# Value bias taken out of the value rows and added to the residual rows on GpSimd

## The chip, the core and the metric

The kernel runs on one core of one Trainium2 chip. A core has five engines with instruction streams of their own: TensorE (PE, matrix multiplications into PSUM), VectorE (DVE), ScalarE (ACT), GpSimd (POOL) and SyncE (SP, which here issues DMAs). They meet through semaphores. SBUF is the working memory of 128 partitions, PSUM holds eight accumulator banks, and DMAs move data to and from HBM. The metric is device time in microseconds (us) of one execution.

## The reference, cut to what matters

32 images are cut into patches and projected to 192 channels, reordered to 256 tokens along a Hilbert curve, and joined by 77 text tokens: 333 tokens of 192 channels an image (B = 32, L = 333, D = 192). Then:

```python
q = layernorm(h)
key = pointwise(depthwise(q)) + pw_b          # 9 taps, 12 heads of 16 channels
kern = einsum(key * q, ak_w) + ak_b           # 9 scores for each token and head
w = softmax(kern, axis=-1)                    # over the 9 taps: sums to 1
v = q @ pt_w.T + pt_b                         # the values and their bias
vp = pad(v, 4 zero rows on both sides)        # the padding is put on after the bias
out[l] = sum_k w[l, k] * vp[l + k]            # window of 9 tokens
h = h + out
h = h + ffn(layernorm(h))                     # 8 experts, top 2, capacity 1598
```

Since the nine weights sum to one, the bias can be left out of v and added once to h, if the rows of the padding hold minus the bias.

## The kernel before, in words

There are two stages. The second (the experts, from about 785 us) isn't touched. The first has two interleaved parts. Part one works on pairs of images (pair p, 16 pairs; buffers alternate with p % 2): TensorE projects the patches (patch), VectorE adds the token bias and takes statistics (norm), GpSimd makes scale and offset of them (pair_norm), ScalarE normalises (normalise), TensorE transposes, ScalarE copies the transposed tiles out (tiles_out). For each of three tiles t TensorE runs the convolution (conv) and the value projection (values). attend(p, t) on VectorE then adds the pointwise bias and multiplies by the query (L605), and adds the value bias ptb_sb to the one value bank bankV while it moves it to the row buffer (L610). scores and scores_out make the 9 x 12 scores. SyncE stores the row buffer (values, hidden row, scores) in the DRAM tensor token_rows (store).

Part two works on groups of four images (group g, 8 groups, two buffers): load_window reads scores (kb), values with a margin of four rows on both sides (vx) and the hidden rows (hg) back in another layout, 11 tokens to a partition. VectorE runs the softmax (softmax_top L632 to L636, ScalarE's exponential, softmax_end) and the window in two slices of 6 and 5 tokens: for each of nine taps a product (L652) and an addition to hg (L670), so that hg becomes the residual sum. Then statistics, a layer norm through GpSimd (slice_norm) and ScalarE (normalise_slice), halves in 16 bits (high_parts on ScalarE, low_parts on GpSimd), the router (logits, top_two, counts_before, offsets, places) and 22 indirect DMAs a group that GpSimd issues (scatter).

No planner sets the order: each engine's program is written out by hand in one loop over it = 0 to 7, in which it handles pairs 2 it and 2 it + 1, the softmax of group it - 1 and the tail of group it - 2. VectorE fills the time between two attends with pieces of the window (part). Each engine takes its instructions strictly in that order, so a wait holds up all that stands behind it. The margins of token_rows are written once from the tile zeros by three DMAs that ScalarE issues; the same engine issues fill(0) and fill(1), 16 large DMAs that preset the expert slots, in iteration 0.

In the last iteration the group 7 has no pairs beside it: TensorE sums the first slice's taps (L1015, L1019), and GpSimd's order is low_parts(6, 0), scatter(5, 0), slice_norm(6, 1), scatter(5, 1) and so on.

## Time and profile before

| | us |
|---|---|
| median of 3 runs | 1483.41 (1480.34 to 1488.11) |
| profiled execution, time | 1478.12 |
| profiled execution, span | 1476.2 |
| busy PE, DVE, ACT, POOL | 1249.6, 991.2, 449.7, 715.1 |

Busy times are sums over the whole span; shares differ much between the two stages, so stretches are read one by one. In rows of instructions, the first number is the start in us from the span's start, the second the busy time (of all merged into the row), then engine, line and operation, output and inputs, shape, and how many instructions were merged; in brackets stands how long the engine had been idle before and what released it. An engine name with a q (ACTq, SPq) is its issuing side. L12 is line 12 of the kernel.

### The profile page before, as it was taken

What the parts mean: (1) busy time and instruction counts of PE and PEld (TensorE: products, weight loads), DVE (VectorE), ACT (ScalarE), POOL (GpSimd) and SP (SyncE); (2) the same over time, 40 slices, a digit from 0 to 9 for tenths busy, and PEclk for the clock granted to TensorE, in tenths of its full rate; (3) what the DMA queues carried; (4) which work ended last, traced back from release to release, by engine and by line L of the source; (5) the groups of instructions that cost most, each with busy time, mean ns of one, the idle gap of its engine ahead of it and who ended that gap; (6) DMA issues with size and microseconds to landing.
All of it is one profiled execution on the core that took longest, in us unless ns stands there. A gap on an engine that the chain in (4) does not pass through costs nothing. (4 is left out here: it accounts for less than half of the span.)

```text
span 1476.2 us, 23362 instructions
## 1 busy us (share of the span) xinstructions
PE 1249.6 (85%) x8476; PEld 991.4 (67%) x8476; DVE 991.2 (67%) x1924; ACT 449.7 (30%) x949; POOL 715.1 (48%) x545
## 2 busy tenths in 40 slices
PE   6969888988989798843640999999999999999994
PEld 6757666777767576533330787787777778877873
DVE  4107959999999999997841565656564655656552
ACT  2011222223232222212031443434442434344331
POOL 1000221766666665746376345545556255455455
PEclk9989998999989898765755999999999999999997
DMA  9795563655656554623024455464656365554533
GB/s 328 299 357 154 134 175 87 183 150 158 180 161 171 153 139 110 155 74 100 23 69 122 84 79 89 62 111 55 103 61 106 58 100 64 91 78 61 71 46 36
DMA packets 224279, 178.52 MB, mean 121 GB/s; under 512 B 128872, under 2 KB 208006, under 8 KB 224160
## 3 DMA queue, kind: packets, MB, share of 16 engines
q1 hardware_dynamic: 176896, 117.16, 32.7%
q0 software_dynamic: 37248, 36.15, 16.1%
q10 hardware_dynamic: 10016, 23.66, 4.3%
q8 instruction: 70, 1.15, 0.3%
q14 instruction: 49, 0.40, 0.1%
HBM read 69.22 MB, written 89.23 MB: 107 GB/s over the span
## 5 line engine op out<-in xcount | busy, mean ns | idle before, releaser
L1127 POOL DMA_INDIRECT out<-yb,meta x200 | 329.4, 1647 | 323.2 <-DVE yb L1184 252.2
L1216 DVE TENSOR_TENSOR hidden<-silu,bankU 128x320 f32<-128x320 f32 x320 | 155.2, 487 | 198.0 <-PE bankU L1249 172.7
L902 PE MATMUL bankK<-normedT,conv_w 128*128 128x333 f32 x864 | 278.7, 471 | 0.0
L85 POOL DMA_INDIRECT expert_inputs<-slot_rows,slots x176 | 230.0, 1307 | 78.4 <-issue 55.0
L1156 ACT ACTIVATE silu<-bankG 128x320 f32<-128x320 f32 x320 | 139.8, 437 | 379.7 <-PE bankG L1249 358.4
L902 PEld LDWEIGHTS bankK<-normedT,conv_w 128*128 128x128 f32 x864 | 169.5, 202 | 78.0 <-issue 13.1
L1262 PE MATMUL bankY<-w_high,hidden_high 128*128 128x192 f16 x800 | 197.2, 246 | 0.0
L1263 PE MATMUL bankY<-w_low,hidden_high 128*128 128x192 f16 x800 | 197.2, 246 | 0.0
L1264 PE MATMUL bankY<-w_high,hidden_low 128*128 128x192 f16 x800 | 197.2, 246 | 0.0
L652 DVE TENSOR_TENSOR prod<-window_values,kb 128x960 f32<-128x960 f32 (+1 forms) x135 | 168.3, 1255 | 3.6
L670 DVE TENSOR_TENSOR hidden_group<-hidden_group,prod 128x960 f32<-128x960 f32 (+1 forms) x135 | 169.1, 1253 | 0.5
L352 POOL TENSOR_TENSOR tmp<-mean_var,pool_constants 128x6 f32<-128x6 f32 (+1 forms) x32 | 25.3, 791 | 250.5 <-DVE mean_var L597 230.2
L880 PE MATMUL bankH<-wp_sb,patches 128*128 128x192 f32 x768 | 131.6, 333 | 10.1 <-DMA tokb_sb<-in_tokb 10.1
L880 PEld LDWEIGHTS bankH<-wp_sb,patches 128*128 128x128 f32 x768 | 128.2, 195 | 10.1 <-DMA tokb_sb<-in_tokb 10.1
L1207 DVE TENSOR_TENSOR hidden_low<-hidden,hidden_high 128x640 f16<-128x640 f32 x160 | 131.6, 822 | 2.2
L1245 PE MATMUL bankG<-xeT,w_high 128*128 128x320 f16 x320 | 96.3, 301 | 39.8 <-DMA xeT<-expert_inputs 36.3
L1150 ACT CAST hidden_high<-hidden 128x640 f16<-128x640 f32 x160 | 115.0, 719 | 8.8 <-DVE hidden L1216 8.8
L1184 DVE TENSOR_SCALAR yb<-bankY,slot_weight 128x192 f32<-128x192 f32 x200 | 75.8, 413 | 62.2 <-PE bankY L1264 62.0
L1245 PE MATMUL bankU<-xeT,w_high 128*128 128x320 f16 x320 | 96.3, 301 | 4.6 <-DVE hidden L1216 4.6
L1248 PE MATMUL bankG<-xeT,w_high 128*128 128x320 f16 x320 | 96.4, 301 | 0.0
L1246 PE MATMUL bankG<-xeT,w_high 128*128 128x320 f16 x320 | 96.4, 301 | 0.0
L1247 PE MATMUL bankG<-xeT,w_low 128*128 128x320 f16 x320 | 96.3, 301 | 0.0
(131 smaller groups left out, 2212.7 us busy)
## 6 DMA issues: line engine op xcount, KB each, us to landing
patches<-in_x SPq DMA_DIRECT2D x16, 1536.0 KB, 8.6
token_rows<-rowbuf SPq DMA_DIRECT2D x32, 492.0 KB
expert_inputs<-prod ACTq DMA_DIRECT2D x8, 1470.0 KB, 15.0
window_values<-token_rows SPq DMA_DIRECT2D x32, 264.0 KB, 5.5
hidden_group<-token_rows SPq DMA_DIRECT2D x32, 264.0 KB, 7.1
expert_inputs<-prod ACTq DMA_DIRECT2D x8, 980.0 KB, 16.6
window_values<-token_rows SPq DMA_DIRECT2D x32, 192.0 KB, 5.7
kb<-token_rows SPq DMA_DIRECT2D x32, 148.5 KB, 4.7
```

The costliest lines, as they stand in the source:

```text
L85: nc.gpsimd.indirect_dma_start(out=xslots[:, :], out_offset=bass.IndirectOffsetOnAxis(ap=idx[g % 2][:, k, r:r + 1], axis=0), in_=xrow[g % ...
L652: return V.tensor_tensor(to[:, 0:(hi - lo) * D].rearrange("p (a d) -> p a d", d=IPG), vx[g % 2][:, (lo + k) * D:(hi + k) * D].rearrange("p ...
L670: added[k] = done(V.tensor_tensor(acc, acc, prod[k % 2][:, 0:(hi - lo) * D], ALU.add))
L880: mm = T_.matmul(bankH[c][:, m * D:(m + 1) * D], xb[u][:, m, kc * TI + c * 128:kc * TI + c * 128 + 128], wp_sb[:, kc, :], start=(kc == 0), ...
L902: mm = T_.matmul(bankK[(u + t) % 2][:, 0:L], conv_w[:, t // 2, k, :], qT[u][:, t, k:k + L], start=(k == 0), stop=(k == K - 1))
L1127: nc.gpsimd.indirect_dma_start(out=out[:, :], out_offset=bass.IndirectOffsetOnAxis(ap=meta[t % NMETA][:, c, 0:1], axis=0), in_=yb[v][:, c, ...
L1156: nc.scalar.activation(sg[m][:, :], bankG[m][:, 0:HALF], ACT.Silu, scale=1 / WSCALE).then_inc(silu_done, 1)
L1216: V.tensor_tensor(hf[j % 2][:, m * HALF:(m + 1) * HALF], sg[m][:, :], bankU[m][:, 0:HALF], ALU.mult).then_inc(prod_done, 1)
L1245: T_.matmul(o, wh[ee][:, lo:lo + 128], high, start=True, stop=False)
L1262: T_.matmul(o, hh[v][:, j, cs], wh[ee][:, ws], start=(j == 0), stop=False)
L1263: T_.matmul(o, hh[v][:, j, cs], wl[ee][:, ws], start=False, stop=False)
L1264: mm = T_.matmul(o, hl[v][:, j, cs], wh[ee][:, ws], start=False, stop=(j == NJ - 1))
```

## The change

The bias leaves attend: VectorE no longer touches the value bank. values_out on ScalarE copies it (three for each pair, at six places of ScalarE's loop). The margin rows are filled with minus the bias, which VectorE writes into the tile zeros first; their three DMAs move from the front of ScalarE's program to iteration 0, behind the first tile copies. bias_rows(g) on GpSimd adds the bias to the 11 residual rows of each partition, in place, once hg is loaded; VectorE's first window addition and, in the last group, TensorE wait for it. GpSimd waits for the constants before its first work. The bias constant is loaded once instead of twice side by side.

```diff
--- before.py
+++ after.py
@@ -101,7 +101,7 @@
             akB_sb = sb("akB_sb", [128, 2 * HB * K])
             ptA_sb = sb("ptA_sb", [128, D])
             ptB_sb = sb("ptB_sb", [128, 2 * D])
-            ptb_sb = sb("ptb_sb", [128, 2 * D])
+            ptb_sb = sb("ptb_sb", [128, D])
             conv_w = sb("conv_w", [128, 2, K, 128])
             xb = [sb(f"patches{u}", [128, 2, KC * TI]) for u in range(2)]
             rowb = [sb(f"rowbuf{u}", [128, 3, 2, ROW]) for u in range(2)]
@@ -168,7 +168,7 @@
             const_loaded = sem("const_loaded")
             zeroed = sem("zeroed")
             empty_set = sem("empty_set")
-            margins_done = sem("margins_done")
+            margin_set, margins_done = sem("margin_set"), sem("margins_done")
             fill_done = sem("fill_done")
             x_loaded = [sem(f"x_loaded{u}") for u in range(2)]
             txt_loaded = [sem(f"txt_loaded{u}") for u in range(2)]
@@ -192,6 +192,7 @@
 
             vk_loaded = [sem(f"vk_loaded{b}") for b in range(2)]
             hg_loaded = [sem(f"hg_loaded{b}") for b in range(2)]
+            hg_biased = sem("hg_biased")
             step = sem("vector_step")
             sc_ready, sc_exp = sem("sc_ready"), sem("sc_exp")
             weights_done = sem("weights_done")
@@ -211,7 +212,7 @@
 
             CONSTS = [(idn[:, :], ident), (wp_sb[:, :, :], wpatch), (tokb_sb[:, :], tokb), (dw_sb[:, :, :], dw),
                       (pw_sb[:, :, :], pw), (pwb_sb[:, :], pwb), (akA_sb[:, :], akA), (akB_sb[:, :], akB),
-                      (ptA_sb[:, :], ptA), (ptB_sb[:, :], ptB), (ptb_sb[:, :], ptb),
+                      (ptA_sb[:, :], ptA), (ptB_sb[:, :], ptB), (ptb_sb[:, :], ptb[:, 0:D]),
                       (akb_sb[:, :], akb), (wgA[:, :], wg[0:128, :]), (wgP[:, :], wgpair), (wgC[:, :], wg[D2:D, :]), (low_sb[:, :], lower),
                       (rev[:, :], revrank), (val[:, :], valid), (sbase[:, :], slotbase), (tid[:, :], tokid)]
             NFIRST = 3
@@ -389,9 +390,19 @@
                         pool.wait_ge(scattered, 16 * NSC * (g + 1))
                         pool.sem_inc(rows_sent, 1)
 
+                def bias_rows(g):
+
+                    pool.wait_ge(hg_loaded[g % 2], loads(g, 1))
+                    nc.gpsimd.tensor_tensor(hg[g % 2][:, :, :], hg[g % 2][:, :, :],
+                                            ptb_sb[:, :].unsqueeze(1).to_broadcast([128, R, D]), ALU.add)\
+                        .then_inc(hg_biased, 1)
+
+                pool.wait_ge(const_loaded, NCONST)
                 pair_norm(0)
                 for it in range(NG):
                     pair_norm(2 * it + 1)
+                    if it:
+                        bias_rows(it - 1)
                     if it > 1:
                         low_parts(it - 2, 0)
                     if it > 2:
@@ -407,6 +418,7 @@
                     if it:
                         slice_norm(it - 1, 0)
                 low_parts(NG - 2, 0)
+                bias_rows(NG - 1)
                 scatter(NG - 3, 0)
                 slice_norm(NG - 2, 1)
                 scatter(NG - 3, 1)
@@ -423,15 +435,6 @@
             def _(act):
                 for dst, src in CONSTS[NFIRST:]:
                     act.dma_start(dst, src).then_inc(const_loaded, 16)
-                act.wait_ge(zeroed, 1)
-                act.dma_start(rows[:, 0:PAD, :], zeros[0:B].unsqueeze(1).to_broadcast([B, PAD, ROW]))\
-                   .then_inc(margins_done, 16)
-                tail = LROWS - PAD - L
-                act.dma_start(rows[:, PAD + L:LROWS, :], zeros[0:B].unsqueeze(1).to_broadcast([B, tail, ROW]))\
-                   .then_inc(margins_done, 16)
-                act.dma_start(out[N:N + 2 * SLOT_TILE, :].rearrange("(p j) d -> p j d", p=CHUNK),
-                              zeros[0:CHUNK, 0:D].unsqueeze(1).to_broadcast([CHUNK, 2 * SLOT_TILE // CHUNK, D]))\
-                   .then_inc(margins_done, 16)
                 tiles = xslots.rearrange("(e t p j) f -> e p t (j f)", t=TPE, p=CHUNK, e=E)
 
                 def fill(q):
@@ -441,6 +444,26 @@
                             act.dma_start(tiles[e][:, v::2, :], prod[v][:, 0:EMPTY].bitcast(u16).unsqueeze(1)
                                           .to_broadcast([CHUNK, (TPE + 1 - v) // 2, SLOT_TILE // CHUNK * XW]))\
                                .then_inc(fill_done, 16)
+
+                def margins():
+
+                    act.wait_ge(margin_set, 1)
+                    act.dma_start(rows[:, 0:PAD, :], zeros[0:B].unsqueeze(1).to_broadcast([B, PAD, ROW]))\
+                       .then_inc(margins_done, 16)
+                    tail = LROWS - PAD - L
+                    act.dma_start(rows[:, PAD + L:LROWS, :], zeros[0:B].unsqueeze(1).to_broadcast([B, tail, ROW]))\
+                       .then_inc(margins_done, 16)
+                    act.dma_start(out[N:N + 2 * SLOT_TILE, :].rearrange("(p j) d -> p j d", p=CHUNK),
+                                  zeros[0:CHUNK, D:2 * D].unsqueeze(1).to_broadcast([CHUNK, 2 * SLOT_TILE // CHUNK, D]))\
+                       .then_inc(margins_done, 16)
+
+                def values_out(p, t):
+                    u, T = p % 2, CT[t]
+                    act.wait_ge(v_ready, 3 * p + t + 1)
+                    if t == 0:
+                        wait(act, row_stored[u], 64 * (p // 2))
+                    nc.scalar.copy(rowb[u][0:T, t, :, 0:D],
+                                   bankV[0:T, 0:2 * D].rearrange("p (m d) -> p m d", m=2)).then_inc(v_evac, 1)
 
                 def normalise(p):
                     u = p % 2
@@ -515,18 +538,28 @@
                 tiles_out(0)
                 for it in range(NG):
                     p = 2 * it
+                    if it == 0:
+                        margins()
+                    values_out(p, 0)
+                    values_out(p, 1)
                     normalise(p + 1)
                     if it == 0:
                         act.wait_ge(empty_set, 2)
                         fill(0)
+                    values_out(p, 2)
                     if it:
                         exponentials(it - 1)
                     tiles_out(p + 1)
                     scores_out(p)
                     if it > 1:
                         normalise_slice(it - 2, 1)
+                    values_out(p + 1, 0)
                     if it > 1:
-                        routing_out(it - 2, 0, NQ)
+                        routing_out(it - 2, 0, 3)
+                    values_out(p + 1, 1)
+                    if it > 1:
+                        routing_out(it - 2, 3, NQ)
+                    values_out(p + 1, 2)
                     if not last(p + 1):
                         normalise(p + 2)
                     if it == 0:
@@ -605,13 +638,6 @@
                     V.scalar_tensor_tensor(ca[u][:, t, :], bankK[(u + t) % 2][:, 0:L],
                                            pwb_sb[:, t // 2:t // 2 + 1], qT[u][:, t, PAD:PAD + L],
                                            ALU.add, ALU.mult).then_inc(ca_done, 1)
-                    T = CT[t]
-                    dve.wait_ge(v_ready, 3 * p + t + 1)
-                    V.tensor_tensor(rowb[u][0:T, t, :, 0:D],
-                                    bankV[0:T, 0:2 * D].rearrange("p (m d) -> p m d", m=2),
-                                    ptb_sb[0:T, :].rearrange("p (m d) -> p m d", m=2), ALU.add)\
-                        .then_inc(v_evac, 1)
-
 
                 counted = [0]
 
@@ -674,7 +700,7 @@
                         mult(k)
                         yield
                         if k == 1:
-                            dve.wait_ge(hg_loaded[g % 2], loads(g, 1))
+                            dve.wait_ge(hg_biased, g + 1)
                         add(k - 1)
                         yield
                     add(K - 1)
@@ -778,6 +804,7 @@
                 dve.wait_ge(first_loaded, 16 * NFIRST)
                 norm(0)
                 dve.wait_ge(const_loaded, NCONST)
+                V.tensor_scalar(zeros[:, 0:D], ptb_sb[:, :], -1.0, None, ALU.mult).then_inc(margin_set, 1)
                 for t in range(2):
                     for k in range(K):
                         ins = V.tensor_scalar(conv_w[:, t, k, :], pw_sb[:, t, :], dw_sb[:, t, k:k + 1], None, ALU.mult)
@@ -848,7 +875,7 @@
                         dve.wait_ge(tap_summed, k - 1)
                     tap(g, 0, k, prodL[k % 2]).then_inc(tap_made, 1)
                     if k == 1:
-                        dve.wait_ge(hg_loaded[g % 2], loads(g, 1))
+                        dve.wait_ge(hg_biased, g + 1)
                     if k == 3:
                         top_two(h)
                     if k == 6:
@@ -1007,7 +1034,7 @@
                 g, h = NG - 1, NG - 2
                 for _ in logits(h, NPAIR):
                     pass
-                pe.wait_ge(hg_loaded[g % 2], loads(g, 1))
+                pe.wait_ge(hg_biased, g + 1)
                 pe.wait_ge(ca_done, 3 * NPAIR)
                 pe.wait_ge(h_in_rows, 2 * NPAIR)
                 hgf = hg[g % 2][:, :, :].rearrange("p r d -> p (r d)")
```

## Rows read from the trace of the kernel before

**Rows 1.** The page's 40 slices of the span, VectorE, busy tenths.

```profile
DVE  4107959999999999997841565656564655656552
```

**Rows 2.** VectorE's waits, 200 to 760 us: total us, times, longest us.

```profile
DVE conv_attn L605 <- PE bankK L902: 14.7, 2, 13.3
...
DVE rowbuf L610 <- PE bankV L916: 3.0, 5, 1.1
```

**Rows 3.** VectorE's instructions in order of time, iteration 6 and behind the loop.

```profile
503.50 0.56 DVE L605 SCALAR_TENSOR_TENSOR conv_attn<-bankK,pwb_sb,normedT 128x333 f32<-128x333 f32 x1
...
511.29 1.40 DVE L632 TENSOR_TENSOR kb<-kb,akb_sb 128x1188 f32<-128x1188 f32 x1 [0.23 <-DMA window_values<-token_rows]
512.72 1.39 DVE L634 TENSOR_REDUCE kmax<-kb 128x132 f32<-128x1188 f32 x1
514.15 2.60 DVE L636 TENSOR_TENSOR kb<-kb,kmax 128x1188 f32<-128x1188 f32 x1
...
517.14 0.54 DVE L610 TENSOR_TENSOR rowbuf<-bankV,ptb_sb 77x384 f32<-77x384 f32 x1
517.61 1.14 DVE L670 TENSOR_TENSOR hidden_group<-hidden_group,prod 128x960 f32<-128x960 f32 x1
...
569.59 0.17 DVE L735 TENSOR_TENSOR off<-bankN,base 128x16 f32<-128x16 f32 x1
...
583.09 0.56 DVE L605 SCALAR_TENSOR_TENSOR conv_attn<-bankK,pwb_sb,normedT 128x333 f32<-128x333 f32 x1
...
669.31 2.59 DVE L670 TENSOR_TENSOR hidden_group<-hidden_group,prod 128x960 f32<-128x960 f32 x1
```

**Rows 4.** Instructions in order of time at the start, TensorE's, then ScalarE's.

```profile
94.35 0.82 PE L892 MATMUL bankT<-identity,normed 128*128 128x128 f32 x3 [10.84 <-ACT normedT L464]
...
37.39 7.76 ACTq L441 DMA_DIRECT2D expert_inputs<-prod  x4
51.78 0.78 ACT L464 COPY normedT<-bankT 128x333 f32<-128x333 f32 x2 [15.04 <-PE bankT L892]
...
82.16 11.60 ACTq L441 DMA_DIRECT2D expert_inputs<-prod  x3
```

**Rows 5.** VectorE's instructions in order of time, start and tail.

```profile
45.16 0.56 DVE L610 TENSOR_TENSOR rowbuf<-bankV,ptb_sb 128x384 f32<-128x384 f32 x1 [0.73 <-PE bankV L916]
...
82.97 0.55 DVE L610 TENSOR_TENSOR rowbuf<-bankV,ptb_sb 77x384 f32<-77x384 f32 x1 [0.73 <-PE bankV L916]
...
694.67 1.39 DVE L642 TENSOR_REDUCE ksum<-kb 128x132 f32<-128x1188 f32 x1 [8.44 <-ACT kb L508]
```

**Rows 6.** ScalarE's instructions in order of time, iteration 6.

```profile
537.82 0.48 ACT L504 COPY xTr<-bankT 128x384 f32<-128x384 f32 x1
...
551.10 3.57 ACT L453 ACTIVATE normed<-rowbuf,rstd 128x192 f32<-128x192 f32 x9
```

**Rows 7.** TensorE's instructions in order of time, iterations 5 and 6.

```profile
487.06 0.40 PE L969 MATMUL bankN<-cnt,lower_sb 128*128 128x16 f32 x2 [3.17 <-DVE cnt L728]
...
554.85 0.74 PE L892 MATMUL bankT<-identity,normed 128*128 128x128 f32 x6
```

**Rows 8.** GpSimd's instructions in order of time, iteration 6 and behind the loop.

```profile
512.98 0.91 POOL L375 TENSOR_TENSOR slot_rows<-group_normed,slot_rows 128x384 f16<-128x384 f32 x1
513.85 1.64 POOL L376 TENSOR_TENSOR slot_rows<-group_normed,slot_rows 128x768 f16<-128x768 f32 x1
...
668.34 2.55 POOL L376 TENSOR_TENSOR slot_rows<-group_normed,slot_rows 128x768 f16<-128x768 f32 x1
671.06 1.76 POOL L85 DMA_INDIRECT expert_inputs<-slot_rows,slots  x1 [0.17 <-issue]
```

**Rows 9.** SyncE's DMA issues in order of time, iteration 6.

```profile
506.50 1.20 SPq L281 DMA_DIRECT2D hidden_group<-token_rows  x2
```

**Rows 10.** One line's instructions: min/median/max ns; DMA landing of L281; issues of L441.

```profile
DMA to landing us min/median/max: 6.0/7.1/13.7
...
L441 ACTq DMA_DIRECT2D expert_inputs<-prod x16: 373/1336/6192, 33.2 to 87.6; - x16
```

## The prediction

> **What bounds the kernel now.** I read the slice table first, then the waits of VectorE, then the instructions of one iteration in order of time on each engine. The slice table [rows 1] has VectorE at four, one and no tenths in its first three slices (36.9 us each, to 111 us), at nine or more in the fifth and in the seventh to eighteenth, and at four to six from the 21st on: the expert stage, which the change doesn't touch and which I carry over unchanged. The waits of VectorE between 200 and 760 us [rows 2] are small: 14.7 us for the convolution bank in two waits (one of 13.3 us when iteration 2 turns to its second pair) and 3.0 us for the value bank. So from about 216 to 620 us VectorE sets the pace; one iteration (4 images) runs from the key evacuation at 503.50 to the one at 583.09, 79.6 us [rows 3]. Before 216 us it is TensorE's chain, and that waits for ScalarE: at 94.35 us TensorE had stood 10.84 us for a transposed tile [rows 4], which ScalarE could copy only after it had issued the fill DMAs. After 682 us it is a chain through GpSimd and ScalarE, for which VectorE stands 8.44 us [rows 5]. An off-loading of VectorE can therefore gain only in the middle, and costs on ScalarE and GpSimd count at both ends.
>
> **Part 1: 48 bias additions leave VectorE.** In rows 3 such an addition starts at 517.14 and the next instruction at 517.61: it holds VectorE 0.47 us, not its 0.54. Six per iteration give 2.8 us. In the VectorE-bound part lie 33 of the 48 (three of iteration 2, six in each of iterations 3 to 7): 33 x 0.47 = 15.5 us, and 3.0 us of waiting for the value bank [rows 2] goes with them. Upper bound of the gain: 18.5 us. The other 15 stand beside TensorE's chain and give nothing.
>
> **Part 2: 48 copies on ScalarE.** A copy of 384 columns from PSUM takes 0.48 us [rows 6], 2.9 us per iteration on an engine with gaps; the price is order, not time. (a) values_out(p+1, 2) now stands ahead of normalise(p+2). Before, that normalise ran 551.10 to 554.67 [rows 6], beside TensorE's convolution, and the transposes began at 554.85 [rows 7]. Now it waits until the last value bank is full (about 554.9), copies for 0.5 and then runs 3.6 us: TensorE's transposes start some 4.3 us later. What hides it: at the same place TensorE stands 3.17 us for the counts [rows 7] (the row of the iteration before), so 1.2 us is left over, and VectorE, now some 1.4 us sooner there by three additions, has no more room before it wants the counts' result at 569.59 [rows 3]. (b) values_out(p+1, 0) stands behind normalise_slice(it-2, 1), which GpSimd's later slice_norm will hold up (part 3): about another 1 us for TensorE.
>
> **Part 3: bias_rows on GpSimd, 8 instructions of 128 x 2112.** The trace shows no such instruction. Its rate I take from low_parts: 384 columns start at 512.98 and the 768 columns behind them take 1.64 us against 0.91 [rows 8], so 0.73 us per 384, 1.90 ns a column; 2112 columns give 4.2 us. The Trainium skill, "GPSIMD Engine Reference", section 3.1, gives a fp32 tensor_tensor of 2048 columns as 4497 ns; by it this would be an estimated 4.6 us, and the sum 2 to 3 us higher. Far more than its own length counts what it does to VectorE. The subtraction of the maxima reads two tensors of SBUF and starts at 514.15; it takes 2.60 us [rows 3], while GpSimd's low_parts runs 513.85 to 515.49 [rows 8], though the addition of the same shape just before takes 1.40. At 669.31 a window addition takes 2.59 us [rows 3] instead of 1.14, beside low_parts again [rows 8]. The reduction at 512.72 [rows 3], with one input, isn't held up by the smaller low_parts instruction. So VectorE instructions with two SBUF inputs and GpSimd's elementwise ones exclude each other. This is what the Trainium skill says in "SBUF — State Buffer", on the shared port pair: whoever starts first holds it for its whole instruction, and the other blocks fully. By this rule the offered relief is paid back on the same engine.
> When does bias_rows start? The last residual rows are issued at 506.50, the second of two a little after, and take 7.1 us in the median [rows 9, 10]: 513.5 to 514.5, when pair_norm is just through (512.98). It then runs to about 517.7. VectorE is in its reduction until 514.1 and wants the subtraction: it waits 3.5 us. If the subtraction wins instead, the window addition behind it waits as long. Bounds: 0 us (the bias falls wholly beside reductions, PSUM reads and statistics) to 4.2 + 1.1 us. I take 3.5. low_parts, which cost the subtraction 1.2 us, moves behind it and stands before the window addition at 517.61 instead: up to 2.2, I take 1.9, so 0.7 more.
>
> **One iteration.** On VectorE: -2.8 - 0.2 (value waits) + 3.5 + 0.7 = +1.2 us. On TensorE the copies of the next pair's tiles follow the exponential, which follows the subtraction, so TensorE moves back 2.3 us with VectorE; then come the 1 us of (b) and the 4.3 of (a) less 3.17 idle: the counts' result is ready 4.5 us later than before, about 0.9 to 2.8 us after VectorE wants it (the higher end if the idle time lowers the granted clock during the patch matmuls). Both together: +3.2 us an iteration, between -1 (no block at all, only the order on ScalarE) and +5. Iterations 3 to 6: 12.8 us. Iteration 7 has no next pair to transpose: +2. Iterations 1 and 2: the blocks of VectorE lie before its wait of 13.3 us, and what TensorE waited for the value bank pays for its new stall: 0.
>
> **The start.** The margins leave ScalarE's queue before its first work and come where it is idle: 0. But in iteration 0, values_out(0, 1), which can't run before 45.2 us (the addition at 45.16 shows when that bank is full [rows 5]), now stands ahead of normalise(1) and fill(0). Before, the fill's issues began at 33.2 [rows 10] and their last four took 7.76 us to 45.15, well before the tile copies at 51.78 [rows 4]. Now they begin at 45.2, and the tile copies wait for them: if they take 7 to 12 us, to 52.5 to 57.2, TensorE loses 1 to 6 us; I take 3.5. In the second half values_out(1, 2) (82.97 [rows 5], now 86.5) stands ahead of normalise(2) and fill(1). That fill's issues began before 82.16, where its last three took 11.60 us to 93.8, and the tile copies for which TensorE stood until 94.35 came right behind [rows 4]. Now they begin at about 86.5 on quieter DMA queues; with 12 to 17 us of issue the copies come at 98.5 to 103.5, 5 to 10 later than before in total. I take +7 for the start, between +2 (the fills issue freely) and +11. Nothing takes it back, since TensorE leads until 216 us.
>
> **The tail.** bias_rows(7) stands between low_parts(6, 0) and scatter(5, 0), which began at 671.06 [rows 8]. Its rows land at about 672, it may wait a window instruction, and ends near 677. Behind the seven scatters come slice_norm, normalise_slice, three tile copies and the exponential for which VectorE stood until 694.67 [rows 5]: that chain is the critical one and takes the delay whole, 6 us, unless a pause in the scatters takes up to 3 of it. I take +5 (2 to 6).
>
> **Sum.** 7 + 0 + 12.8 + 2 + 5 = +26.8 us. The profiled execution took 1478.1 (span 1476.2), giving 1505; the median shown is 1483.4, giving 1510. I set the base between them, at 1481, and predict 1508 us. A change under 0.5% (7.4 us) can't be told from none here.
>
> **Rivals.** (R1) GpSimd and VectorE don't exclude each other for this instruction, or it falls beside one-input work: then start 4, four iterations at -1, iteration 7 at -2 and tail 3, +1; 1482 us. For it: I have only shapes up to 768 columns. Against: two different VectorE instructions are stretched by the length of GpSimd's. (R2) The other side: VectorE was the bound and its relief goes through. The point from which it decides is a block under 3.0 us an iteration (what VectorE saves) with TensorE's stall inside its idle time; with no block, fills that issue freely (2) and a tail of 3, minus the 18.5 of part 1: -13.5; 1468 us. For it: TensorE stands 3.17 us behind the moved normalise, so most of its stall may be hidden. Against: the block alone is above the 3.0. (R3) The start dominates: the fills come into the store and load traffic of the pairs and their issue takes 17 us or more each time, while the blocks cost as forecast and TensorE drops to its lower clock at each new stall: start 11, five iterations at 5, tail 6: +42; 1523 us.
>
> **How the numbers follow.** Forecast 0.55 (its own range 1493 to 1521), R1 0.17, R2 0.12, R3 0.16. The range 1480 to 1524 leaves out R2 and the tip of R3. Faster by over 0.5%: R2 and the edge of R1, 0.14. Within 0.5%: most of R1 and the lower edge of the forecast, 0.14. Slower: 0.72.
>
> **What would show it.** Right, if the profile after has eight GpSimd instructions of about 4.2 us; a subtraction of the maxima or a window addition of 4 to 6 us in each of iterations 3 to 7; an iteration of about 82.8 us; TensorE waiting some 4 us for the normalised rows at the transposes of even pairs; and VectorE resuming in the tail some 25 us late. Wrong, if VectorE's two-input instructions keep their 1.16 to 1.40 us during bias_rows, or if the copies after the first fill come by 52 us.

## The result, and the profile after

The changed kernel takes 1529.64 us (median of 5, 1525.43 to 1544.08) against 1483.41: ratio 1.0309, 95% interval 1.0278 to 1.0341, so 46 us slower. The forecast was 1508 with a range up to 1524. The direction and the mechanism hold, the sizes don't.

The profiled execution of the changed kernel is the longest of its five (1544). I read instead a second profile of the same kernel, called again below: median 1529.15, span 1524.4, against a span of 1476.2 before. That leaves 48.2 us to explain. Its slice table, TensorE and VectorE in tenths of 38.1 us, then the granted clock:

```profile
PE   6868888889888888861542599999998999999994
DVE  4015967999989998989682365656565565656552
PEclk9989989998989899885675799999999999999997
```

VectorE's row answers to [rows 1]: its first part has the same shape and is longer. Where the time is lost is plainest from the first key evacuation of each iteration (`conv_attn` instructions 1, 7, 13, ... of VectorE), of its last one, of the last sum of exponentials and of the first load of an expert's weights:

```
us      it0   it1    it2    it3    it4    it5    it6    it7    last   ksum   weights  span
before  37.5  113.3  187.4  263.5  343.7  423.1  503.5  583.1  640.1  694.7  785.4    1476.2
again   38.2  123.8  197.3  283.1  367.9  451.7  536.1  620.8  681.0  740.3  830.7    1524.4
later    0.7   10.5    9.9   19.6   24.2   28.6   32.6   37.7   40.9   45.6   45.3      48.2
```

Ten us go in iteration 0, none in 1, ten in 2, 4 to 5 in each of 3 to 6, 3 in 7, 5 in the tail, and 3 in the expert stage. The last 3 I don't put down to the change, which doesn't touch that stage: before_port and no_add below don't show them, port_beside does.

Inside an iteration (number 4, in order of time, VectorE first, then GpSimd):

```profile
374.65 1.40 DVE L658 TENSOR_TENSOR kb<-kb,akb_sb 128x1188 f32<-128x1188 f32 x1
376.08 1.39 DVE L660 TENSOR_REDUCE kmax<-kb 128x132 f32<-128x1188 f32 x1
377.50 5.56 DVE L662 TENSOR_TENSOR kb<-kb,kmax 128x1188 f32<-128x1188 f32 x1
...
383.46 1.38 DVE L696 TENSOR_TENSOR hidden_group<-hidden_group,prod 128x960 f32<-128x960 f32 x1
384.88 2.49 DVE L678 TENSOR_TENSOR prod<-window_values,kb 128x960 f32<-128x960 f32 x1
```
```profile
377.14 4.66 POOL L396 TENSOR_TENSOR hidden_group<-hidden_group,ptb_sb 128x2112 f32<-128x2112 f32 x1 [0.77 <-DMA hidden_group<-token_rows]
381.76 2.06 POOL L376 TENSOR_TENSOR slot_rows<-group_normed,slot_rows 128x384 f16<-128x384 f32 x1
383.79 2.56 POOL L377 TENSOR_TENSOR slot_rows<-group_normed,slot_rows 128x768 f16<-128x768 f32 x1
```

This is [rows 3] and [rows 8] once more with the new instruction in front. GpSimd starts 0.36 us ahead, and the subtraction, 1.40 us by its shape, ends when GpSimd's 4.66 are over and it has had its own time: 377.14 + 4.66 + 1.40 = 383.2 against 383.06. Both low_parts instructions come behind it and are stretched in their turn (2.06 and 2.56 us against 0.91 and 1.64), and a window product takes 2.49.

Iteration 1 loses nothing, and the reason is a race. There the subtraction starts 0.01 us ahead of GpSimd's addition and keeps its 1.40 us; GpSimd's instruction takes 5.92 us, and of VectorE's instructions only the product at 141.99 is held (2.09 us instead of 1.40). The profile of 1544 us, where GpSimd started first, has 77.2 us for iteration 1 instead of 73.5. From again:

```profile
136.89 1.40 DVE L662 TENSOR_TENSOR kb<-kb,kmax 128x1188 f32<-128x1188 f32 x1
```
```profile
136.90 5.92 POOL L396 TENSOR_TENSOR hidden_group<-hidden_group,ptb_sb 128x2112 f32<-128x2112 f32 x1 [5.17 <-DMA hidden_group<-token_rows]
```

The copies on ScalarE and the transposes behind them, in iteration 4 again:

```profile
423.05 0.47 ACT L465 COPY rowbuf<-bankV 77x384 f32<-77x384 f32 x1 [3.84 <-PE bankV L943]
423.43 3.57 ACT L476 ACTIVATE normed<-rowbuf,rstd 128x192 f32<-128x192 f32 x9
```
```profile
427.05 2.06 PE L919 MATMUL bankT<-identity,normed 128*128 128x128 f32 x9 [4.04 <-ACT normed L476]
428.90 8.99 PE L907 MATMUL bankH<-wp_sb,patches 128*128 128x192 f32 x48
```

TensorE stands 4.04 us where in [rows 7] it went straight on. VectorE's waits over 200 to 760 us (line waited for, total us, times, longest) answer to [rows 2]:

```profile
DVE conv_attn L638 <- PE bankK L929: 20.3, 3, 15.7
DVE off L761 <- PE bankN L997: 10.9, 5, 3.0
...
DVE stats L624 <- DMA rowbuf<-in_txt: 6.1, 5, 1.8
```

The value bank's 3.0 us are gone, and 10.9 us of waiting for the counts are new. At the start, ScalarE and its DMA issues, for [rows 4]:

```profile
45.79 0.48 ACT L465 COPY rowbuf<-bankV 128x384 f32<-128x384 f32 x1 [5.86 <-PE bankV L943]
45.83 0.42 ACTq L444 DMA_DIRECT2D expert_inputs<-prod  x1
...
50.67 7.08 ACTq L444 DMA_DIRECT2D expert_inputs<-prod  x3
57.80 0.47 ACT L465 COPY rowbuf<-bankV 77x384 f32<-77x384 f32 x1 [8.07 <-issue]
58.18 0.77 ACT L487 COPY normedT<-bankT 128x333 f32<-128x333 f32 x2
...
94.71 9.22 ACTq L444 DMA_DIRECT2D expert_inputs<-prod  x4
104.03 0.78 ACT L487 COPY normedT<-bankT 128x333 f32<-128x333 f32 x2 [9.12 <-issue]
```

The tile copies come at 58.18 and 104.03 instead of 51.78 and 93.86. In the tail, VectorE and GpSimd, for [rows 5] and [rows 8]:

```profile
740.32 1.39 DVE L668 TENSOR_REDUCE ksum<-kb 128x132 f32<-128x1188 f32 x1 [9.47 <-ACT kb L531]
```
```profile
711.97 4.81 POOL L396 TENSOR_TENSOR hidden_group<-hidden_group,ptb_sb 128x2112 f32<-128x2112 f32 x1 [0.70 <-DMA hidden_group<-token_rows]
716.95 1.76 POOL L85 DMA_INDIRECT expert_inputs<-slot_rows,slots  x1 [0.17 <-issue]
```

### The profile page after: what moved, and what is told of

It reads as the page before. It is cut to its first block and busy times, and to the rows that moved or that the text cites. A ratio compares the mean times of both kernels' runs of the same rounds, so it can differ in the third digit from the quotient of the medians.

```text
span 1542.3 us, 23386 instructions
## 1 busy us (share of the span) xinstructions
PE 1281.0 (83%) x8476; PEld 1018.6 (66%) x8476; DVE 1005.1 (65%) x1877; ACT 472.0 (31%) x997; POOL 749.0 (49%) x553
## 3 DMA queue, kind: packets, MB, share of 16 engines
q8 instruction: 71, 1.16, 0.3%
## 5 line engine op out<-in xcount | busy, mean ns | idle before, releaser
L85 POOL DMA_INDIRECT expert_inputs<-slot_rows,slots x176 | 215.3, 1223 | 78.5 <-issue 55.0
L678 DVE TENSOR_TENSOR prod<-window_values,kb 128x960 f32<-128x960 f32 (+1 forms) x135 | 179.3, 1337 | 3.6
L907 PE MATMUL bankH<-wp_sb,patches 128*128 128x192 f32 x768 | 156.3, 373 | 10.2 <-DMA tokb_sb<-in_tokb 10.1
L907 PEld LDWEIGHTS bankH<-wp_sb,patches 128*128 128x128 f32 x768 | 153.3, 226 | 10.6 <-DMA tokb_sb<-in_tokb 10.1
L1272 PE MATMUL bankG<-xeT,w_high 128*128 128x320 f16 x320 | 96.5, 302 | 41.7 <-DMA xeT<-expert_inputs 36.8
L638 DVE SCALAR_TENSOR_TENSOR conv_attn<-bankK,pwb_sb,normedT 128x333 f32<-128x333 f32 x48 | 26.9, 560 | 108.8 <-PE bankK L929 106.4
L1273 PE MATMUL bankG<-xeT,w_high 128*128 128x320 f16 x320 | 96.6, 302 | 0.0
```

The lines of the kernel that those rows point to most:

```text
L85: nc.gpsimd.indirect_dma_start(out=xslots[:, :], out_offset=bass.IndirectOffsetOnAxis(ap=idx[g % 2][:, k, r:r + 1], axis=0), in_=xrow[g % ...
L678: return V.tensor_tensor(to[:, 0:(hi - lo) * D].rearrange("p (a d) -> p a d", d=IPG), vx[g % 2][:, (lo + k) * D:(hi + k) * D].rearrange("p ...
L907: mm = T_.matmul(bankH[c][:, m * D:(m + 1) * D], xb[u][:, m, kc * TI + c * 128:kc * TI + c * 128 + 128], wp_sb[:, kc, :], start=(kc == 0), ...
L1272: T_.matmul(o, wh[ee][:, lo:lo + 128], high, start=True, stop=False)
```

## Experiments

Sixteen kernels ran, in four groups, each beside runs of the kernel before on its chip (medians 1484.27, 1479.46, 1483.55, 1478.65). The chips differ, so kernels of different groups are compared by their ratios to before. A period is the time from the first key evacuation of one iteration to that of the next. Theory A: GpSimd's addition and VectorE's two-input instructions exclude each other, and that is most of the loss. Theory B: ScalarE's new order is. Theory C: the relief of VectorE is real and is only paid back.

**again**, the changed kernel unaltered.

> The changed kernel, not altered, for a second profile and as the base of this group. The profiled execution seen so far took 1544 us against a median of 1530; its first stage ended 58.7 us later than before and its expert stage took 7.4 us more. If the extra 14 us were of that execution alone, the new profile has a first stage later by 45 to 50 us and an expert stage as before; 1530 us.

1529.15 us, ratio 1.0318 [1.0285, 1.0351]. The reference for what follows.

**no_add**, GpSimd's addition left out, so the residual rows lack the bias; its semaphore is still raised.

```
-  nc.gpsimd.tensor_tensor(hg, hg, ptb_sb, ALU.add).then_inc(hg_biased, 1)
+  pool.sem_inc(hg_biased, 1)
```

> GpSimd's wait for the residual rows stays, its addition of 128 x 2112 is left out, so the residual rows lack the bias. Port theory (the addition excludes VectorE's instructions with two SBUF inputs): the subtraction of the maxima falls from 5.1 us to 2.2, iterations 2 to 6 from 86 to 82 us and the tail gains 5; 1502 us. Order theory (most of the loss is ScalarE's order): only the tail and TensorE's tile copies move, 1518 us or more.

1500.99 us, 1.0117 [1.0091, 1.0143]. The addition is worth 28 us; 17 stay without it. The ten us of the start stay (first evacuation of iteration 1 at 123.3), and the periods of iterations 3 to 6 are 80.8, 80.3, 81.3 and 79.9, no shorter than before although VectorE does 2.8 us less in each. Iterations 1 and 2 together stay 4.6 us longer than before. All of it comes in iteration 2, where TensorE stands for the normalised rows as in the changed kernel:

```profile
252.12 2.16 PE L917 MATMUL bankT<-identity,normed 128*128 128x128 f32 x9 [4.04 <-ACT normed L474]
```

**pow28**, in its place a power of 28 columns into a scratch tile, about as long as the addition (4.79 us where nothing holds it); the bias is left out.

> In place of the addition GpSimd runs a power over 28 columns of a tile of its own, some 4.6 us long but with next to nothing read; the residual rows lack the bias. It holds GpSimd's queue for as long as the addition did, and not the port. Port theory: VectorE's instructions run as without the addition, and only GpSimd's later work stays late: 1507 us, within 6 us of no_add. Queue theory (the delay comes through GpSimd's later norms and scatters): as slow as the changed kernel, 1528 us.

1519.39 us, 1.0244 [1.0216, 1.0272]. The powers and the subtractions (count | busy us, mean ns | idle before):

```profile
L399 POOL TENSOR_TENSOR busy<-busy 128x28 f32<-128x28 f32 x8 | 42.9, 5359 | 16.4 <-DMA hidden_group<-token_rows 16.3
...
L663 DVE TENSOR_TENSOR kb<-kb,kmax 128x1188 f32<-128x1188 f32 x8 | 11.2, 1396 | 0.3
```

Of iteration 2, GpSimd and then VectorE:

```profile
212.73 4.79 POOL L399 TENSOR_TENSOR busy<-busy 128x28 f32<-128x28 f32 x1 [5.51 <-DMA hidden_group<-token_rows]
```
```profile
212.93 1.40 DVE L663 TENSOR_TENSOR kb<-kb,kmax 128x1188 f32<-128x1188 f32 x1
```

The power blocks nobody: even where it starts first, as here, the subtraction keeps 1.40 us. Yet it costs 18 us over no_add. VectorE now waits 24.3 us in five waits for the counts (10.1 in no_add; this profile is pow28's longest execution, 1527.9). The way leads through ScalarE: the power delays slice_norm, for which normalise_slice waits (8.7 us in iteration 3, 4.2 in no_add), and the copy of the value bank, which the change put behind normalise_slice, comes 1.6 to 4.9 us after the bank is full in iterations 3 to 6 (0.5 us at most in no_add). So in the changed kernel an instruction of this length costs by its place in GpSimd's queue too. How the two costs share the 28 us isn't shown.

**order_both**: the changed kernel with the fills issued ahead of the second value copy and normalise(p+2) ahead of the last one.

> GpSimd's addition stays. ScalarE issues the fills where it did before (normalise(1) and four fill DMAs ahead of the first value copy, fill(1) ahead of the copy of pair 1's last tile), and in every iteration normalises pair p+2 ahead of the copy of pair p+1's last tile. Order theory: the start's 11 us come back, and each iteration loses the 4 us stall of TensorE and the slow patch matmuls behind it, 2 to 3 us of it on the path: 1505 us. Port theory: only the start comes back and 1 us an iteration, 1514 us.

1528.74 us, 1.029 [1.0258, 1.0322]: nothing. In the loop TensorE's stall of 4 us for the normalised rows is gone, but VectorE is still blocked, and the periods don't fall (85.2 on average in iterations 3 to 6 against 84.4 in again, in a profile that is order_both's longest execution). The start is hardly restored (121.7 for iteration 1): the margin DMAs still stand right ahead of the fills.

**start_fix**: the start's order only, with the margins behind the tile copies of pair 1 (condensed; in the second half normalise(2) and fill(1) also go ahead of the last value copy).

```
 if it == 0:
-    margins(); values_out(p, 0); values_out(p, 1); normalise(p + 1); fill(0)
+    normalise(p + 1); fill(0, 0, 2); values_out(p, 0); fill(0, 2, 4); values_out(p, 1)
     values_out(p, 2); tiles_out(p + 1)
+    margins()
```

> The changed kernel with the start of ScalarE's queue put back as far as it goes: normalise(1), four of the first eight fills, the first value copy, the other four, the second value copy; the margin DMAs behind the tile copies of the second pair, so that they no longer stand just ahead of the fills (they did when the start was put back the first time, which gained nothing); in the second half normalise(2) and the second fills ahead of the last value copy. The loop is the changed kernel's. If the start's 10 us come from the fills having been moved behind value copies, the first window addition stage begins 7 to 10 us sooner and the time is 1519 to 1522. If they come from the margins that now share the queues with the fills, wherever they stand, it stays at 1526 to 1530.

1517.41 us, 1.0264 [1.0224, 1.0304]. Iteration 1 begins at 118.8, so half of the start comes back by order: 2.1 us with the fills in their old place (order_both), 2.9 more with the margins out of their way.

**margins_front** (condensed) adds to it the issue, at the very start, of the margins' columns that hold zeros and of the output's zeros.

```
+ edge(D, ROW); act.dma_start(out[N:...], zeros)     # ahead of everything
  ...
+ edge(0, D)                                         # minus the bias, behind the tile copies
```

> start_fix with the margins split: the columns of keys and scores of the margin rows and the zeros of the output (2.05 of 2.62 MB) go out at the very start as before, when the DMA queues stand idle in start_fix (17.5 to 22 us); only the 192 value columns, which hold minus the bias, stay behind the first tile copies (0.58 MB). If the rest of the start's loss is their share of the saturated queues (some 400 GB/s from 35 to 110 us), 2.05 MB are worth 5 us: the first window stage begins at 113.5 to 115 instead of 118.8 and the time is 5 us under start_fix. If it is the value copies in ScalarE's chain, nothing changes: within 1.5 us of start_fix.

Iteration 1 begins at 113.8, where before had 113.3: the other half is bytes. The stretches 17 to 22 and 22 to 110 us of before, start_fix and margins_front (stretch, its length, busy time of PE, PEld, DVE, ACT and POOL with instructions, granted clock, DMA share, GB/s):

```profile
17.00:22.00 5.00, 5.00 (x33) 5.00 (x32) 2.02 (x7) 1.28 (x1) 0.00 (x0) 1.00 0.99 268
22.00:110.00 88.00, 72.84 (x345) 58.35 (x344) 17.37 (x65) 16.73 (x48) 6.18 (x12) 0.92 0.91 332
```
```profile
17.00:22.00 5.00, 5.00 (x33) 5.00 (x32) 2.23 (x8) 0.00 (x0) 0.00 (x0) 1.00 0.28 61
22.00:110.00 88.00, 68.89 (x317) 55.10 (x316) 13.96 (x59) 18.20 (x48) 6.30 (x12) 0.88 0.94 331
```
```profile
17.00:22.00 5.00, 5.00 (x33) 5.00 (x32) 1.93 (x7) 1.28 (x1) 0.00 (x0) 1.00 1.09 341
22.00:110.00 88.00, 72.12 (x345) 57.79 (x344) 14.39 (x61) 19.37 (x54) 6.30 (x12) 0.92 0.91 326
```

Moved to where ScalarE is idle, the margins left an idle stretch of the DMA engines (share 0.28 instead of 0.99) for one in which these are full (0.94 from 22 to 110 us, at 331 GB/s). The whole time is 1514.58, 1.0237 [1.0218, 1.0257], which overlaps start_fix: iteration 2 begins at 192.9 in the one and 192.4 in the other. The 5 us went in iteration 1, by the race seen above. In start_fix the subtraction started first and GpSimd waited; in margins_front GpSimd started first, and the subtraction took 5.73 us. GpSimd's additions of iteration 1 in the two:

```profile
131.98 5.91 POOL L396 TENSOR_TENSOR hidden_group<-hidden_group,ptb_sb 128x2112 f32<-128x2112 f32 x1 [5.39 <-DMA hidden_group<-token_rows]
```
```profile
126.64 4.64 POOL L396 TENSOR_TENSOR hidden_group<-hidden_group,ptb_sb 128x2112 f32<-128x2112 f32 x1 [5.12 <-DMA hidden_group<-token_rows]
```

**before_port**: the kernel before, with GpSimd's addition into a scratch tile that nobody reads, at the place of bias_rows and waited for as there.

```
+ nc.gpsimd.tensor_tensor(scr, hg[g % 2], ptb_sb, ALU.add).then_inc(hg_biased, 1)
- dve.wait_ge(hg_loaded[g % 2], loads(g, 1))
+ dve.wait_ge(hg_biased, g + 1)
```

> The kernel before with one thing added: at the places of bias_rows GpSimd adds 128 x 2112 from the residual rows into a scratch tile that nobody reads (VectorE and TensorE wait for it as in the changed kernel); values, margins and ScalarE's order are those of before. It measures what the GpSimd instruction costs by itself, without any relief or reorder. Port theory (VectorE stands for the 4.65 us, and low_parts meets the window additions behind it): 5 to 6 us in iterations 2 to 7 and 5 in the tail, +32 to +40: 1516 to 1524. If the loop's loss was mostly ScalarE's new order: under +15, below 1499.

1518.86 us, 1.0253 [1.0224, 1.0282], +37 to 39. One instruction per group, with no work taken from VectorE and no order of ScalarE changed, is enough for four fifths of the loss. Its iterations against those of before: -0.3 us in iteration 0, then +6.1, +6.2, +6.7, +6.2, +5.0, +5.4, +1.1 in iteration 7, and +5.3 from the last evacuation to the last sum. All eight of its additions start before VectorE's instruction and stretch it to 5.1 to 5.9 us. Where the time goes in iterations 3 to 6 is read from this stretch in before, before_port, no_add and pow28 (columns as in margins_front):

```profile
263.50:583.10 319.60, 283.74 (x1407) 225.65 (x1406) 303.81 (x558) 92.37 (x228) 205.59 (x169) 0.93 0.56 155
```
```profile
275.50:618.50 343.00, 292.25 (x1413) 234.61 (x1412) 321.84 (x558) 92.45 (x228) 228.74 (x173) 0.90 0.53 144
```
```profile
278.10:600.40 322.30, 284.50 (x1404) 226.54 (x1403) 293.03 (x533) 103.17 (x252) 203.67 (x169) 0.94 0.56 153
```
```profile
282.60:624.00 341.40, 296.83 (x1409) 235.13 (x1408) 298.21 (x534) 102.01 (x252) 223.30 (x173) 0.91 0.55 145
```

The same 558 instructions of VectorE take 18.0 us more (321.84 against 303.81) of the 23.4 by which the stretch is longer, and in it VectorE never waits for the counts. That is the exclusion; the other 5.4 us are waits that I haven't traced. As no_add has the waits for the counts (10.1 us) and before_port hasn't, they come with the moved copies and not with the addition. In pow28, against no_add, it is the other way round: 5.2 us more of busy time, 13.9 us more of waits. Where TensorE leads, the block reaches it through ScalarE's tile copies; these are the transposes that wait for them in iteration 2, before and before_port:

```profile
199.60 0.51 PE L892 MATMUL bankT<-identity,normed 128*128 128x128 f32 x3 [0.88 <-ACT normedT L464]
```
```profile
208.82 0.81 PE L904 MATMUL bankT<-identity,normed 128*128 128x128 f32 x3 [4.17 <-ACT normedT L476]
```

**port_beside**: the same idle instruction, from iteration 2 to 6 released by the first token rows of norm(2it+2).

```
+ if it > 1 and not last(2 * it + 1): pool.wait_ge(h_in_rows, 2 * (2 * it + 2) + 1)
+ if it > 1: bias_rows(it - 1)
  if not last(2 * it + 1): pair_norm(2 * it + 2)
```

> The same idle GpSimd addition of 128 x 2112 into a scratch tile as in before_port, in the kernel before, but from iteration 2 to 6 it starts when VectorE has stored the first token rows of the next pair (h_in_rows of pair 2it+2), so that it runs beside VectorE's norm, whose instructions read at most one tensor of the residual kind from SBUF and one from PSUM (statistics, 3 us and more). Port theory (what costs is the exclusion against two-input instructions of VectorE): the subtraction is back at 1.4 to 2.6 us and an iteration at 79.5 to 81, so before_port's cost falls from 38 to 10 to 16 us (tail 5, iterations 1, 2 and 7 some 5, a late pair_norm 1 per iteration): 1490 to 1496. If the cost is the length of GpSimd's queue, wherever the instruction stands, it stays at 1510 or more.

1499.48 us, 1.0112 [1.0087, 1.0137]: 16 left of 38. In iterations 1 and 7 and in the tail a block remains (5.76, 5.73 and 5.49 us). GpSimd, then VectorE, iteration 5:

```profile
468.86 4.76 POOL L396 TENSOR_TENSOR scratch_rows<-hidden_group,ptb_sb 128x2112 f32<-128x2112 f32 x1 [3.22 <-DVE rowbuf L599]
```
```profile
444.30 2.60 DVE L652 TENSOR_TENSOR kb<-kb,kmax 128x1188 f32<-128x1188 f32 x1
...
468.23 1.01 DVE L599 TENSOR_TENSOR rowbuf<-bankH,tokb_sb 128x384 f32<-128x384 f32 x2
470.43 1.66 DVE L607 BATCH_NORM_STATS2 stats<-rowbuf 128x6 f32<-128x192 f32 x6 [1.18 <-DMA rowbuf<-in_txt]
472.26 0.51 DVE L613 BATCH_NORM_AGGREGATE mean_var<-stats 128x2 f32<-128x6 f32 x6 [0.17 <-DVE stats L607]
472.69 3.47 DVE L668 TENSOR_TENSOR prod<-window_values,kb 128x1152 f32<-128x1152 f32 x2
```

For 4 us both engines work at their own speed (additions from PSUM, statistics); only the last 0.9 us meet a window product. In iterations 3 to 6 the same instruction costs 5 to 7 us in one place and 1 to 3 in the other. The new place also lies behind more of GpSimd's queue, so this run by itself doesn't part exclusion and queue; the busy times of before_port do. So the first half of theory A, the exclusion, is shown, and by itself it can make most of such a loss. In the changed kernel, where the queue costs too, its share isn't shown.

**free_order**: no addition at all (rows lack the bias), start_fix's start, and normalise(p+2) ahead of the last value copy: the most that the relief can bring.

> As start_fix, with GpSimd's addition left out (the residual rows lack the bias) and normalise(p+2) ahead of the last value copy in every iteration. It is the most that moving the 48 value additions to ScalarE can bring. Theory A (VectorE bounds the loop and only ScalarE's order kept its relief back): 15 us less than the kernel before, 1466 to 1474. Theory B (the relief is worth nothing, because TensorE's chain or the landing of the text rows and of the windows comes just behind VectorE): 1480 to 1490, with VectorE waiting in each iteration for what it saves.

1478.50 us against 1479.46, 0.9989 [0.9978, 0.9999]: 1 us instead of 15. Theory C falls for this kernel. Against no_add (1.0117) it also shows what ScalarE's new order and the margins cost once the addition is gone: some 19 us. Theory B has this second part of the loss; beside the addition the loop's order alone brought nothing (order_both). VectorE's instructions with a wait in iteration 5:

```profile
438.37 1.40 DVE L664 TENSOR_TENSOR kb<-kb,akb_sb 128x1188 f32<-128x1188 f32 x1 [1.03 <-DMA window_values<-token_rows]
467.73 1.66 DVE L630 BATCH_NORM_STATS2 stats<-rowbuf 128x6 f32<-128x192 f32 x6 [2.04 <-DMA rowbuf<-in_txt]
```

It waits for what it saves.

**free_txt** and **before_txt**: free_order and before with the statistics of the chunk that holds the text rows taken last, `for c in (0, 1, 2)` for `(2, 0, 1)`.

> As free_order (no addition to the residual rows at all, values on ScalarE), with the statistics of the third row chunk, the only one that needs the text rows from DRAM, taken last instead of first, so that their landing (waits of up to 2.0 us in free_order) is hidden by the statistics of the other two. If the relief of VectorE was eaten by the landing of the text rows: 2 us less in each of five iterations, 10 us under free_order. If TensorE's chain is what stands behind VectorE: no difference, 0 to 3 us.

> The kernel before with the same exchange of the statistics' order and nothing else. VectorE waited there 4.9 us for the text rows in 8 waits: at most 5 us less, more likely 1 to 3; it is the control for free_txt.

0.9969 [0.9952, 0.9987] and 0.9972 [0.9957, 0.9986]: the same in both, 4 to 5 us under before. The periods of iterations 3 to 6 don't show it (79.8 and 80.0 on average), and where the 4 us lie isn't traced. The landing of the text rows was only what VectorE happened to wait for: over 200 to 760 us this wait falls from 7.2 us in free_order to 1.5 in free_txt, and 5.0 us of waits ahead of the offsets (off), which free_order hasn't, take its place.

**before_less** and **free_less**: before and free_order with a quarter of every patch matmul group left out, `for kc in range(3, KC)`.

> The kernel before with 9 instead of 12 contraction steps in every patch matmul group (a quarter of the patch embedding left out; the loads stay), 48 matmuls or 4 us less of TensorE's work per iteration. If VectorE alone bounds the loop of before: the periods of iterations 3 to 6 stay at 79.4 to 80.4. If TensorE shares the bound: 1 to 3 us shorter. Where TensorE leads (iterations 0 to 2) 2 to 4 us per iteration are won either way. The number of tokens per expert may change, so the last key evacuation of the loop is compared, not the whole time.

> free_order with the same quarter of the patch matmuls left out: both engines are relieved. If TensorE stands just behind VectorE, the periods of iterations 3 to 6 fall from 79.5 to 76.5 to 78 (VectorE's 2.8 us now go through), and by clearly more than in before_less. If it is the DMA landings and the exchange of results between the engines, they stay at 79 to 80 in both.

Periods of iterations 3 to 6, in us:

```
                       VectorE as before                 six additions fewer
TensorE as before      80.3 79.4 80.4 79.6  mean 79.9    80.3 78.1 79.7 79.3  mean 79.3
TensorE 4 us less      79.2 79.5 79.3 79.1  mean 79.3    78.9 77.8 77.5 77.4  mean 77.9
```

Relieving one engine gives 0.6 us, relieving both 2.0. These are single profiles: free_txt, with the same relief of VectorE, has 79.8, so the 0.6 isn't clear of the spread, the 2.0 is. The two are level in the loop of before; [rows 2] shows VectorE nearly without waits, which is true, but not that TensorE has room. The remaining 0.8 of the 2.8 us I haven't traced. (The number of tokens per expert changes with the embedding, so whole times aren't compared.)

**vec_add**: free_order with the bias added by VectorE once per group, right behind the subtraction.

```
+ V.tensor_tensor(hg[g % 2], hg[g % 2], ptb_sb, ALU.add).then_inc(hg_biased, 1)
```

> As free_order, with the bias added to the residual rows by VectorE, one addition of 128 x 2112 per group right behind the subtraction of the maxima, in place of GpSimd's. It reads two tensors of SBUF, so some 2.4 us by the rate of the window additions (1.1 us for 960 columns). Where VectorE bounds the loop: six times 2.4 and the tail's 2.4, so 12 to 17 us above free_order; where it doesn't: 3 to 8. Against the changed kernel: 30 us or more less, if what GpSimd's addition costs is the block and its queue.

1482.14 us, 1.0014 [0.9998, 1.0029], 2.35 us for each of the eight: 2.7 us over before, 35 us under start_fix, which ran beside it, and some 45 us under the changed kernel. Its periods of iterations 3 to 6 are those of free_order (79.3 on average), so there the addition on VectorE costs nothing.

**beside_txt**: the changed kernel with free_order's order, bias_rows placed as in port_beside, the last group's addition on VectorE, the text chunk last.

> The changed kernel in the best form that I have: start and loop order of free_order, GpSimd's real addition beside VectorE's norm from iteration 2 to 6 as in port_beside, the last group's addition on VectorE while it waits for the exponential, the text chunk's statistics last. By the port theory it pays only iterations 1, 2 and 7 of the blocks (about 5 each, part of it hidden): 1482 to 1490, level with the kernel before or a little above; a gain over it only if free_txt shows one.

1491.56 us, 1.0057 [1.0037, 1.0078], against vec_add's 1.0014: GpSimd's addition, even in the best place that I found for it, is dearer than VectorE's own.

**final**: vec_add with the margins of margins_front and the text chunk last.

> The best whole kernel that the runs point to: values copied by ScalarE in the order of free_order, the margins split as in margins_front, the bias added once per group by VectorE (vec_add), the statistics of the text chunk last. vec_add was at 1.0014 of before; the margins' 5 us and before_txt's 4 us would make 0.994 to 0.998: 1472 to 1478 against 1480. Theory that nothing but TensorE counts in the loop: only the start's 5 us are won, 0.997 to 1.0.

1476.41 us (12 runs), 0.9979 [0.9968, 0.9990]: it is faster than both kernels, by 2 to 3 us and by some 50. The start is whole (iteration 1 at 114.4, 3 at 263.8) and the last evacuation comes at 636.2 instead of 640.1. But before_txt, which moves nothing to ScalarE, is as good.

## Why the prediction was wrong

The forecast was +26.8 us; the profile called again shows +48.2. By the forecast's own steps, with the measured sizes taken from the table of the result:

- **Part 3, the block: right.** GpSimd's additions take 4.65 to 4.81 us, and one, which the subtraction beat, 5.92 (4.2 forecast from low_parts' 1.90 ns a column; the 4.6 that the Trainium skill, "GPSIMD Engine Reference", section 3.1, led to was nearer, so a rate from 768 columns is too low here). In iterations 2 to 7 the block met the subtraction, where I had put it. In iteration 4 this was held 4.2 us, an addition 0.2 and a window product 1.3, against 0.8 for the subtraction of the same iteration before: +4.9 net, where I had 3.5 + 0.7 = 4.2. As the Trainium skill puts it in "SBUF — State Buffer", the first holds the shared port pair for its whole instruction. For the additions the trace agrees, in both orders (GpSimd first in iteration 4, VectorE first in iteration 1), and in port_beside the statistics and the additions from PSUM don't collide. For the power of pow28 it doesn't, though this reads its two inputs from SBUF as well: it started first at 212.73, for 4.79 us, and the subtraction at 212.93 still took 1.40.
- **The step that failed most: "Iterations 1 and 2: ... 0".** I argued that TensorE's waits there would pay. Measured: +9.1 us for both together in again, and +6.1 and +6.2 in before_port. Two things make it. First, where TensorE leads, its chain goes through VectorE all the same: the subtraction gates the exponential, that the tile copies on ScalarE, those the transposes. In iteration 2 TensorE stands 4.17 us for these copies in before_port, where before had 0.88. A block on the engine with room was a delay of the engine without. Second, TensorE's stall for the normalised rows (part 2, a) isn't paid for either: no_add, without any block, keeps 4.6 of the 9.1 us. That iteration 1 of again lost nothing is the luck of the race there.
- **One iteration: right in kind, its terms too small.** Measured +4.6, +4.4, +4.0 and +5.1 in iterations 3 to 6 where I said 3.2, at the end of the bounds (-1 to +5): 18.1 instead of 12.8, and 3.2 instead of 2 in iteration 7. VectorE's busy time rises from 76.0 to 78.0 us an iteration (I had +1.4, from 3.5 + 0.7 - 2.8), and its waits from 4.0 to 6.5, of which 2.2 are those for the counts (0.9 to 2.8 forecast). The relief of 2.8 - 0.2 is in this sum, but it isn't worth its length: without a block it brought 0.6 us an iteration (free_order), and again's mean period is 84.4 against 85.7 in before_port, which has the block and no relief.
- **The start: right in kind, at the end of its range.** 9.8 instead of 7. By start_fix, half of it is the order of fills and margins in ScalarE's queue. The other half is a line that I booked at 0, "the margins leave ScalarE's queue ... and come where it is idle": I asked whether ScalarE was idle, not whether the DMA queues were. They were where the margins stood before, and aren't there (margins_front).
- **The tail: right.** +4.7 against +5. GpSimd's addition at 711.97, the scatters behind it, and the chain behind them takes it whole.
- **Part 2, b, put at 1 us, is the way by which the queue costs:** pow28 shows the value copy behind normalise_slice up to 4.9 us late. What it costs in the changed kernel itself isn't shown.
- **The sum:** 2.8 (start) + 9.1 + 5.3 + 1.2 - 0.3 (tail) make 18.1 of the missing 21.4; 0.7 come before the first evacuation, 2.9 in the expert stage, and -0.3 between.
- **The rivals.** R1 (no exclusion) and R2 (the relief goes through) are out, R2 even with no block at all. R3's total (+42) was near, its reason not: the issues of eight fills take 12 and 13 us, not 17. Of its parts, the start at 11 and the iterations at 5 were near the measured 9.8 and 4.0 to 5.1. The granted clock in iteration 4 is 0.92 against 0.94 before, and the patch matmuls behind TensorE's stall ran 8.99 us against 8.01; this is a part of the 4.5 that I haven't separated. My range ended at R3's tip. The dearer ends of my own terms (11, four times 5, 2 and 6) make +39, 1520; what lay beyond them was the term put at 0.

## What to carry to other kernels

An engine that shows no waits is the bound only if the next one has room: before booking a relief, look for the second engine's busy share in the same stretch (TensorE 70 of 80 us here), and book the relief at zero until both are relieved. Price an elementwise instruction on GpSimd by which VectorE instruction it will meet, and by what stands behind it in GpSimd's own queue; the same 4.7 us cost 6 us beside a two-input subtraction and 1 to 3 beside statistics. Which of two such instructions waits can hang on 0.01 us, so a single profile can show an iteration without its block. A DMA that is moved needs an idle place on the DMA queues, not only on the engine that issues it.

## What was not expected of the hardware

- The exclusion goes both ways in a chain: GpSimd's 384-column instruction took 2.06 us instead of 0.91, and the window product beside it 2.49 instead of 1.16. Each waited for the other's whole instruction, so the long one shifted the meetings of the short ones behind it.
- A power of 28 columns holds GpSimd as long as an addition of 2112 (4.79 us against 4.65) and takes nothing from VectorE, though VectorE takes from it: where the subtraction had started up to 0.05 us earlier, the power took 5.99 to 6.04 us.
